# Counting the edges of a graph layer by tiles instead of by windows

## The chip, the cores and the metric

The kernel runs on one core of a Trainium2 chip. The metric is the device time of one launch in microseconds (us). TensorE, VectorE, ScalarE and GpSimd work side by side and order themselves by semaphores; SyncE (SP) only issues DMAs.

## The reference

1250 nodes with 512 features; 21,250 edges, sorted by `dst`. A softmax over each node's edges weighs its neighbours, then a spline layer, a residual and a layer norm follow. Cut to what matters here:

```python
s = HW @ a[:OUT_F, 0];  t = HW @ a[OUT_F:, 0]          # HW = h @ W
e = leaky_relu(s[row] + t[col])                        # row = src, col = dst
m = segment_max(e, row);  ex = exp(e - m[row]);  den = segment_sum(ex, row)
agg = segment_sum((ex / den[row])[:, None] * h[col], row)
out = silu(agg) @ base_w.T + einsum('nip,oip->no', b_splines(agg), spline_w)
return layernorm(x + out)
```

## The kernel before

The softmax is dense. The kernel counts how often each pair (src, dst) occurs, as a matrix C of 1250 x 1250 (src in 128 partitions x 10 groups j, dst along the columns), with Z a second matrix that is large where C is zero. Then `greatest(j)` (L601) takes for each src the largest t among its neighbours, ScalarE makes the exponentials for all pairs, `weigh` multiplies by C, TensorE transposes and aggregates with x, and after that come 36 units of matmuls of the spline layer (L1113), which fill the time from about 170 us on. This document is about what stands ahead of `greatest(0)`.

**The count.** The edges, sorted by dst, lie in 168 tiles of 128, an edge per partition. C's columns are cut into 40 windows of `DW` = 32 dst, so 320 columns of PSUM (src group x dst). For a window w a fixed run of 7 or 8 tiles, from `FIRST[w]`, is visited: 304 matmuls at L1013, each with a stationary one-hot `still` (edge x 128, L414) and a moving one-hot `oh` (edge x 320, L394). The moving one-hot says src group and dst within a window and is made once for each batch of 8 tiles (`moving`, 21 batches). The stationary one-hot says the low seven bits of src and, in its key, which window the edge belongs to, so that it is zero for edges of other windows; it is made anew for each window (`one_hot_still`, 40 times). Both come from VectorE's `is_equal` of a row of numbers (`im`, `iq`) with keys made from the edges (`mk`, `qk`). Four batches of `oh` and four windows of `still` are held. ScalarE copies each window from PSUM to C (L792) and makes Z (L795); six PSUM banks are in use for windows.

**Tiles left over.** Edges of a window that lie in tiles outside its fixed run are added by a loop on VectorE, TensorE and PSUM bank 7 ahead of `greatest(0)` (L559 to L578). Its trip counts are read from a table that VectorE computes between the one-hots (`least_and_most` to `left_sizes`): least and largest dst of each tile, and from them the tiles that each window still wants. With nothing left over, the loop body runs once.

**s and t.** `w_times_a`, `wa_column` and `st_rows` on TensorE make W a and then two rows, s and t, of 1280 nodes in three chunks (12 matmuls at L989, chunk after chunk, each into partitions 0 and 1 of bank 6). `s_column` turns s into a column; `t_spread` spreads t over all 128 partitions by three matmuls (L1005), which ScalarE copies into `trow`. `greatest(0)` reads trow.

**Order of the work.** It is written out by hand: each engine's program is a loop over windows, with the small pieces of work hung on chosen windows (`WA_AT`, `ST_AT`, `SC_AT`, `TB_AT`, `RG_AT`, `RR_AT`). VectorE also makes `x_low` (L502), ten remainders x - xh, four of them inside the loop and six behind it. GpSimd fills constants at the start, then waits for xT (`s_xt`) and issues two DMAs for `xh` (L362, L363), then waits for the first `greatest` to issue weights (L374). SP issues the loads; its next waiting instruction is also behind the first `greatest`.

```python
for v in range(VIS[w]):
    m = e.matmul(PS[:, w % 6, 0:MV], still[:, w % RH, v, :], oh[:, (FIRST[w] + v) % (RB * TB), :],
                 start=(v == 0), stop=(v == VIS[w] - 1))
```

## Time and profile before

| | |
|---|---|
| time, median of 3 | 429.96 us (428.74 to 430.42) |
| the profiled execution | 430.31 us, of which the span is 428.5 |
| mean granted TensorE clock | 0.979 |
| busy: TensorE, VectorE, ScalarE, GpSimd | 399.4, 367.2, 274.0, 33.1 us |
| start of `greatest(0)` | 76.24 us |

The span runs from the first to the last instruction; the time of a launch is 1.8 us longer. PE is TensorE's matmuls, PEld its weight loads, DVE VectorE, ACT ScalarE, POOL GpSimd. Matmuls overlap their successors, so a group's mean duration is longer than its pace.

### The profile page before, as it was taken

Reading aid. Unit: us, or ns where it says so; the run is one execution under the profiler, and the core shown is the slowest. Engines: PE = TensorE matmul, PEld = TensorE weight load, DVE = VectorE, ACT = ScalarE, POOL = GpSimd, SP = SyncE. Lnnn points to the kernel's source line nnn. Section 1 sums busy time; section 2 is a strip of 40 time slices with the busy share of each in tenths; the row PEclk is TensorE's granted clock in tenths of the full one; section 3 lists DMA queues with packets and bytes.
Section 4 is the critical chain, followed back from the end, with each engine's and each line's share of the span. In section 5 each row is a group of like instructions: output and inputs, shape, how many; then the busy total and the mean of one; then the engine's idle time right before and its main releaser. Section 6 shows DMA issues by size and latency. Waiting matters only on the chain.

```text
span 428.5 us, 5227 instructions
## 1 busy us (share of the span) xinstructions
PE 399.4 (93%) x1881; PEld 306.0 (71%) x1881; DVE 367.2 (86%) x457; ACT 274.0 (64%) x299; POOL 33.1 (8%) x162
## 2 busy tenths in 40 slices
PE   3999995299999999999999999999999999999994
PEld 0436563288888888878778888888777777777772
DVE  7968999997868867799988999989799969999645
ACT  7535675456456659788659586678646785779212
POOL 5100000100000000001100110101011010101000
PEclk9999999589999999999999999999999999999998
DMA  8980000600000000955454636363242346371303
GB/s 265 376 201 2 2 0 0 198 0 2 0 0 2 1 2 6 337 173 144 151 165 134 192 102 194 113 182 89 67 139 50 98 124 194 101 217 50 98 1 115
DMA packets 23452, 45.91 MB, mean 107 GB/s; under 512 B 1831, under 2 KB 2043, under 8 KB 23427
## 3 DMA queue, kind: packets, MB, share of 16 engines
q0 software_dynamic: 11088, 21.44, 18.6%
q1 hardware_dynamic: 12338, 24.14, 17.9%
q8 instruction: 15, 0.25, 0.2%
q14 instruction: 11, 0.08, 0.1%
HBM read 43.02 MB, written 2.56 MB: 106 GB/s over the span
## 4 chain that ended last, share of the span: by engine, by line
PE 54%; issue 29%; DVE 9%; POOL 3%; DMA 3%; ACT 0%; DVEq 0%; POOLq 0%
PE PS L1113 24%; PE PS L1069 17%; PE PS L1013 5%; POOL wh L374 3%; PE PS L1052 3%; DVE still L414 2%; DMA wh<-in_splT 2%; PE PS L989 2%; DVE oh L394 1%; DVE xl L502 1%; PE PS L968 1%; PE PS L1079 1%; DVE wl L593 1%; DMA ei<-in_edges 1%; DVE ex L629 0%
## 5 line engine op out<-in xcount | busy, mean ns | idle before, releaser
L1113 PE MATMUL PS<-wh,s 128*128 128x512 f32 (+1 forms) x720 | 225.2, 392 | 2.3 <-ACT s L884 1.1
L1113 PEld LDWEIGHTS PS<-wh,s 128*128 128x128 f32 (+1 forms) x720 | 133.4, 185 | 36.4 <-ACT s L884 3.5
L1113 PE MATMUL PS<-wl,s 128*128 128x512 f32 (+1 forms) x360 | 141.1, 392 | 0.0
L884 ACT ACTIVATE s<-v 128x1280 fp32r<-128x1280 f32 (+1 forms) x32 | 40.0, 1250 | 63.9 <-DVE v L701 58.9
L1113 PEld LDWEIGHTS PS<-wl,s 128*128 128x128 f32 (+1 forms) x360 | 66.8, 185 | 15.2
L1013 PE MATMUL PS<-oh,still 128*128 128x320 bf16 x304 | 45.4, 304 | 9.9 <-DVE still L414 7.9
L695 DVE SCALAR_TENSOR_TENSOR v<-v,v 128x1280 f32<-128x1280 f32 (+1 forms) x32 | 46.5, 1454 | 4.8 <-ACT v L870 4.8
L1013 PEld LDWEIGHTS PS<-oh,still 128*128 128x128 bf16 x304 | 28.8, 99 | 29.6 <-DVE still L414 9.6
L701 DVE SCALAR_TENSOR_TENSOR v<-v,v 128x1280 f32<-128x1280 f32 (+1 forms) x32 | 46.8, 1461 | 3.3
L711 DVE SCALAR_TENSOR_TENSOR s<-v,s 128x1280 fp32r<-128x1280 f32 (+1 forms) x32 | 46.5, 1454 | 0.6 <-ACT s L884 0.6
L697 DVE SCALAR_TENSOR_TENSOR v<-v,v 128x1280 f32<-128x1280 f32 (+1 forms) x32 | 46.5, 1454 | 0.0
L867 ACT ACTIVATE v<-xt,bias 128x1280 f32<-128x1280 f32 (+1 forms) x32 | 42.9, 1342 | 3.5 <-DVE s L711 2.1
L374 POOL DMA_DIRECT2D wh<-in_splT x32 | 22.8, 714 | 279.8 <-PE PS L1113 170.6
L870 ACT ACTIVATE v<-v,bias 128x1280 f32<-128x1280 f32 (+1 forms) x32 | 42.4, 1326 | 0.0
L868 ACT ACTIVATE v<-xt,bias 128x1280 f32<-128x1280 f32 (+1 forms) x32 | 42.4, 1325 | 0.0
L593 DVE TENSOR_TENSOR wl<-wring,wh 128x1024 fp32r<-128x1024 f32 x24 | 29.2, 1221 | 10.4 <-issue 10.4
L394 DVE TENSOR_TENSOR oh<-im,mk 128x2560 bf16<-128x2560 f16 x21 | 31.0, 1478 | 0.1
L414 DVE TENSOR_TENSOR still<-iq,qk 128x1024 bf16<-128x1024 uint16 (+1 forms) x40 | 25.4, 653 | 5.9 <-PE PS L1013 5.9
L792 ACT CAST C<-PS 128x320 uint16<-128x320 f32 x40 | 17.0, 425 | 20.1 <-PE PS L1013 19.5
L652 DVE TENSOR_TENSOR pl<-PS,ph 128x1280 fp32r<-128x1280 f32 (+2 forms) x11 | 15.1, 1368 | 14.7 <-ACT ph L833 14.7
L1069 PE MATMUL PS<-xh,ph 128*128 128x512 f32 x100 | 27.6, 425 | 0.0
L833 ACT CAST ph<-PS 128x1280 fp32r<-128x1280 f32 (+2 forms) x11 | 12.4, 1132 | 21.4 <-PE PS L1052 21.4
(125 smaller groups left out, 374.4 us busy)
## 6 DMA issues: line engine op xcount, KB each, us to landing
wh<-in_splT POOLq DMA_DIRECT2D x32, 512.0 KB, 4.5
wring<-in_splT SPq DMA_DIRECT2D x21, 512.0 KB, 4.4
xt<-in_xT SPq DMA_DIRECT2D x1, 2500.0 KB, 11.6
xn<-in_x SPq DMA_DIRECT2D x1, 2304.0 KB
xh<-in_x POOLq DMA_DIRECT2D x1, 2304.0 KB, 13.3
out<-xr SPq DMA_DIRECT2D x9, 256.0 KB
wh<-in_baseT POOLq DMA_DIRECT2D x4, 512.0 KB, 5.3
wring<-in_baseT SPq DMA_DIRECT2D x3, 512.0 KB, 4.1
```

Source lines behind the costliest of these rows:

```text
L374: e.dma_start(wh[u % NWS][:, :, :], w_source(u)).then_inc(s_wh[u % NWS], 16)
L695: e.scalar_tensor_tensor(out=ba, in0=bw, scalar=2.0, in1=ba, op0=ALU.subtract, op1=ALU.mult, reverse0=True).then_inc(s_a3, 1)
L697: e.scalar_tensor_tensor(out=bq, in0=bw, scalar=2.0, in1=bq, op0=ALU.subtract, op1=ALU.mult).then_inc(s_b3, 1)
L701: e.scalar_tensor_tensor(out=bw, in0=bq, scalar=2 / 3, in1=ba, op0=ALU.add, op1=ALU.min).then_inc(s_spl, 1)
L711: e.scalar_tensor_tensor(out=parts(sl, u), in0=bufs(u)[0], scalar=0.0, in1=parts(sh, u).bitcast(F32), op0=ALU.max, op1=ALU.subtract).then_ ...
L867: e.activation(bw, agg_in, ACT.Abs, bias=bias[:, q - 1:q], scale=2.5).then_inc(s_abs, 1)
L868: e.activation(bq, agg_in, ACT.Square, bias=bias[:, NP + q - 1:NP + q], scale=2.5 * sq2).then_inc(s_q2, 1)
L870: e.activation(ba, bw, ACT.Square, bias=bias[:, 2 * NP:2 * NP + 1], scale=-sq6).then_inc(s_a2, 1)
L884: e.activation(parts(sh, u), bufs(u)[0], ACT.Relu).then_inc(s_shi, 1)
L1013: m = e.matmul(PS[:, w % 6, 0:MV], still[:, w % RH, v, :], oh[:, (FIRST[w] + v) % (RB * TB), :], start=(v == 0), stop=(v == VIS[w] - 1))
L1069: m = e.matmul(PS[:, 5 + j % 2, :], pp[0:r, j % 3, place(j, t), :], xs[0:r, t, :], start=(i == 0 and t == 0), stop=(i == 2 and t == NT - 1))
L1113: m = e.matmul(PS[0:rows(w), w % 8, :], sx[:, ic, tl * 128:tl * 128 + rows(w)], wx[:, ic, :], start=first and n == 0, stop=last and n == 2)
```

## The change

The windows of the output become 25 of 50 dst (500 columns of PSUM, ordered dst x src group, so column = 10 x dst + group). A tile of edges is counted once: its moving one-hot covers a constant stretch of columns around `middle(t)`, `REACH` columns to either side (90 to 160), and the matmul goes to those columns of one window, or is split in two at a window's border. The stationary one-hot is of the low seven bits of src alone and is made once for each batch. Since no matmul covers a whole window, a matmul with zeros (`cleared`) opens each. Keys relative to the middle of the tile (`mk`) take the place of those relative to a window.

The table of left-over tiles is computed by GpSimd in a chain of 29 steps (`s_tab`), of which VectorE does three (two reductions of the tiles' ends, one reduction at batch 10, one scan at batch 13) and reads the result at batch 17. Ahead of it GpSimd makes keys for left-over edges in ten steps (`s_left`). Both stand behind its xh DMAs. A tile is left over if its first or last dst lies outside its stretch.

`st_rows` puts the three chunks into partitions 0, 32 and 64 of one bank, after batches 7 to 10, with one contraction chunk each time; ScalarE copies them to `strow`, and three DMAs on SP's queue, ahead of its weights, copy the rows of t from there to all partitions of `trow`. The remainders of x start at batch 16.

```diff
-DW = 32
-ND = RP // DW
-MV = NT * DW
+DW = 50
+ND = N // DW
+CW = DW * NT
+MV = LW * NT
 TB = 8
 NB = NC // TB
+NV = NC - 1
 RB = 4
-VIS = [8 if ND // 5 <= w < ND - ND // 5 else 7 for w in range(ND)]
-FIRST = [min(max(((2 * w + 1) * DW * PER_NODE // 2 + 64 - 64 * VIS[w]) // 128, 0), NC - VIS[w]) for w in range(ND)]
-NR = 2 * ND
+MID, PER_TILE, PER_BATCH = 42, 75, 602
+REACH = [5 * (18, 22, 24, 26, 28, 30, 30, 32, 32, 32, 32)[min(b, NB - 1 - b)] for b in range(NB)]
+def middle(t):
+    return MID + PER_BATCH * (t // TB) + PER_TILE * (t % TB)
+def stretches(t):
+    lo, hi = max(middle(t) - REACH[t // TB], 0), min(middle(t) + REACH[t // TB], ND * CW)
+    return [(w, max(lo, CW * w), min(hi, CW * w + CW)) for w in range(lo // CW, (hi - 1) // CW + 1)]
+FIRST_TILE = [min(t for t in range(NV) if w in [p[0] for p in stretches(t)]) for w in range(ND)]
+LAST_TILE = [max(t for t in range(NV) if w in [p[0] for p in stretches(t)]) for w in range(ND)]
...
+            for k, (lo, hi) in enumerate(TCH):
+                hi = min(hi, N)
+                if k == 0:
+                    e.wait_ge(s_srow, 3)
+                e.dma_start(trow[:, lo:hi], strow[32 * k + 1:32 * k + 2, 0:hi - lo].unsqueeze(1).broadcast_to([1, 128, hi - lo])
+                            ).then_inc(s_trow, 16)
...
+            e.wait_ge(s_edge, 16)
+            e.wait_ge(s_bits, 2)
+            e.wait_ge(s_setup, SETUP["reach"])
+            e.tensor_copy(left_place[:, :], ei[:, 1, :]).then_inc(s_left, 1)
+            e.tensor_copy(left_in[:, :], et[:, 0, :]).then_inc(s_left, 1)
...
+            e.tensor_tensor(left_key[:, :, :], left_place[:, :].unsqueeze(2).broadcast_to([128, NCP, 2]),
+                            left_in[:, :].unsqueeze(2).broadcast_to([128, NCP, 2]), ALU.add).then_inc(s_left, 1)
...
+            e.wait_ge(s_ends_r, 1)
+            e.tensor_scalar(wf[:, :, 0:NC], ends[:, :, :], 1 / LW, (1 - LW) / (2 * LW), ALU.mult, ALU.add).then_inc(s_tab, 1)
+            for k in range(2):
+                e.wait_ge(s_tab, k + 1)
+                e.tensor_scalar(wf[:, :, 0:NC], wf[:, :, 0:NC], (WHOLE, -WHOLE)[k], None, ALU.add).then_inc(s_tab, 1)
...
+            e.tensor_scalar(rest[:, 0:NC], n_of[:, :], 1.0, None, ALU.max).then_inc(s_tab, 1)
+            for k in range(2):
+                e.tensor_tensor(ways[:, k, :], ways[:, k, :], out_of[:, :], ALU.mult).then_inc(s_tab, 1)
+            e.wait_ge(s_least, 1)
+            e.tensor_scalar(tu[:, 2:3], tu[:, 0:1], -1.0, float(NC), ALU.mult, ALU.add).then_inc(s_tab, 1)
+            e.wait_ge(s_tab, 16)
...
+            e.wait_ge(s_scan, 1)
+            e.tensor_tensor(here[:, 1, :], wf[:, 0, :], upto_rest[:, 0:NC + 1], ALU.subtract).then_inc(s_tab, 1)
+            e.wait_ge(s_tab, 23)
+            e.tensor_copy(r_rest[:, :, 0], here[:, 1, :]).then_inc(s_tab, 1)
+            for k in range(2):
+                e.tensor_copy(r_rest[:, :, 1 + k], upto_rest[:, k:k + NC + 1]).then_inc(s_tab, 1)
+            e.tensor_copy(r_size[:, 0:1], tu[:, 2:3]).then_inc(s_tab, 1)
+            e.tensor_copy(r_size[:, 1:2], tu[:, 4:5]).then_inc(s_tab, 1)
+            e.tensor_copy(r_size[:, 2:3], upto_rest[:, NC + 1:]).then_inc(s_tab, 1)
...
             def moving(b):
-                c0 = TB * b
+                h = REACH[b]
                 if b >= RB:
-                    e.wait_ge(s_cw, last_window(b - RB) + 1)
+                    e.wait_ge(s_ct, done(b - RB))
                 e.tensor_tensor(
-                    oh[:, c0 % (RB * TB):c0 % (RB * TB) + TB, :].rearrange("p k (m b) -> p k m b", b=2),
-                    im[:, :].rearrange("p (m b) -> p m b", b=2).unsqueeze(1).broadcast_to([128, TB, MV // 2, 2]),
-                    mk[:, c0:c0 + TB, :].unsqueeze(2).broadcast_to([128, TB, MV // 2, 2]),
+                    oh[:, b % RB, :, 0:2 * h].rearrange("p k (m b) -> p k m b", b=2),
+                    im[:, MV // 2 - h:MV // 2 + h].rearrange("p (m b) -> p m b", b=2).unsqueeze(1)
+                    .broadcast_to([128, TB, h, 2]),
+                    mk[:, TB * b:TB * b + TB, :].unsqueeze(2).broadcast_to([128, TB, h, 2]),
                     ALU.is_equal).then_inc(s_mv, 1)
...
-            def one_hot_still(w):
-                k = VIS[w]
-                if w >= RH:
-                    e.wait_ge(s_cw, w - RH + 1)
-                e.wait_ge(s_iq, w.bit_length())
-                e.tensor_tensor(still[:, w % RH, 0:k, :].rearrange("p k (m b) -> p k m b", b=2),
-                                places_of(slice(128 * w, 128 * w + 128), k), lows_of(FIRST[w], k), ALU.is_equal
+            def places_of(k):
+                return im[:, MV // 2:MV // 2 + 128].rearrange("p (m b) -> p m b", b=2).unsqueeze(1).broadcast_to(
+                    [128, k, 64, 2])
+            def one_hot_still(b):
+                e.tensor_tensor(still[:, b % RB, :, :].rearrange("p k (m b) -> p k m b", b=2), places_of(TB),
+                                lk[:, TB * b:TB * b + TB, :].unsqueeze(2).broadcast_to([128, TB, 64, 2]), ALU.is_equal
                                 ).then_inc(s_head, 1)
...
+            e.tensor_scalar(et[:, 0, :], ei[:, 0, :], 7, None, ALU.arith_shift_right).then_inc(s_bits, 1)
+            e.tensor_scalar(et[:, 1, :], ei[:, 0, :], 127, None, ALU.bitwise_and).then_inc(s_bits, 1)
+            e.wait_ge(s_setup, SETUP["mid"])
+            e.wait_ge(s_bits, 1)
+            e.tensor_tensor(left_hi[:, :], et[:, 0, :], mid[:, :], ALU.subtract).then_inc(s_hc, 1)
+            e.wait_ge(s_hc, 1)
+            e.scalar_tensor_tensor(out=mk[:, :, :], in0=ei[:, 1, :].unsqueeze(2).broadcast_to([128, NCP, 2]),
+                                   scalar=float(NT), in1=left_hi[:, :].unsqueeze(2).broadcast_to([128, NCP, 2]),
+                                   op0=ALU.mult, op1=ALU.add).then_inc(s_mk, 1)
+            e.wait_ge(s_mk, 1)
+            for b in range(NB):
+                moving(b)
+                if b == 0:
+                    e.wait_ge(s_lk, 1)
+                one_hot_still(b)
+                if b == 1:
+                    e.wait_ge(s_dn, 16)
+                    e.tensor_reduce(mm[0:NBLK, :, 0], dn[0:NBLK, :, :], AX.X, ALU.min).then_inc(s_ends, 1)
+                    e.tensor_reduce(mm[0:NBLK, :, 1], dn[0:NBLK, :, :], AX.X, ALU.max).then_inc(s_ends, 1)
+                if b == LEAST_AT:
+                    e.wait_ge(s_tab, 15)
+                    e.tensor_reduce(tu[:, 0:2], ways[:, :, :], AX.X, ALU.max).then_inc(s_least, 1)
+                if b == SCAN_AT:
+                    e.wait_ge(s_tab, 22)
+                    e.wait_ge(s_setup, SETUP["begin"])
+                    e.tensor_tensor_scan(upto_rest[:, 1:], rest[:, :], zero[:, :], 0.0, ALU.add, ALU.add
+                                         ).then_inc(s_scan, 1)
+                if b == SIZES_AT:
+                    e.wait_ge(s_tab, TABLE)
+                    first, behind = loaded(e, r_size, 0, 2, 0, NC + 1)
+                if b in X_LOW_AT:
+                    x_low(X_LOW_AT[b] - 1)
+            for k in range(len(X_LOW_AT), NT):
+                x_low(k)
+            e.wait_ge(s_left, 10)
...
+            e.wait_ge(s_bits, 2)
+            e.copy(lk[:, :, :], et[:, 1, :].unsqueeze(2).broadcast_to([128, NCP, 2])).then_inc(s_lk, 1)
+            def st_rows():
+                e.wait_ge(s_sr, 1)
+                for k, (lo, hi) in enumerate(TCH):
+                    e.copy(strow[32 * k:32 * k + 2, 0:hi - lo], PS[32 * k:32 * k + 2, 6, 0:hi - lo]).then_inc(s_srow, 1)
+            def evacuate_counts(w):
+                ps = PS[:, w % 6, 0:CW].rearrange("p (b a) -> p a b", a=NT)
                 d = slice(DW * w, DW * w + DW)
-                e.wait_ge(s_cw, w + 1)
+                e.wait_ge(s_ct, LAST_TILE[w] + 1)
...
-                m.then_inc(s_sr, 1)
+                for k, (lo, hi) in enumerate(TCH):
+                    m = e.matmul(PS[32 * k:32 * k + 2, 6, 0:hi - lo], wa[:, it, :], xt0[:, it, lo:hi], start=(it == 0),
+                                 stop=(it == 3))
+                if it == 3:
+                    m.then_inc(s_sr, 1)
...
-            for w in range(ND):
-                if w >= 6:
-                    e.wait_ge(s_hole, w - 5)
-                e.wait_ge(s_head, w + 1)
-                for v in range(VIS[w]):
-                    m = e.matmul(PS[:, w % 6, 0:MV], still[:, w % RH, v, :], oh[:, (FIRST[w] + v) % (RB * TB), :],
-                                 start=(v == 0), stop=(v == VIS[w] - 1))
-                m.then_inc(s_cw, 1)
-                if w in WA_AT:
-                    w_times_a(WA_AT.index(w))
-                if w == WT_AT:
...
+            def cleared(w):
+                e.matmul(PS[:, w % 6, 0:CW], nought[:, 0:128], nought[:, :], start=True, stop=False)
+            e.wait_ge(s_setup, SETUP["nought"])
+            for w in range(6):
+                cleared(w)
+            for b in range(NB):
+                e.wait_ge(s_mv, b + 1)
+                e.wait_ge(s_head, b + 1)
+                for t in range(TB * b, done(b)):
+                    o = middle(t) - REACH[b]
+                    for w, lo, hi in stretches(t):
+                        if w >= 6 and t == FIRST_TILE[w]:
+                            e.wait_ge(s_hole, w - 5)
+                            cleared(w)
+                        m = e.matmul(PS[:, w % 6, lo - CW * w:hi - CW * w], still[:, b % RB, t % TB, :],
+                                     oh[:, b % RB, t % TB, lo - o:hi - o], start=False, stop=(t == LAST_TILE[w]))
+                    m.then_inc(s_ct, 1)
+                if b in WA_AT:
+                    w_times_a(WA_AT.index(b))
```

## Rows read from the trace of the kernel before

**Rows 1.** table of stretches: length, busy us (x) of PE, PEld, DVE, ACT, POOL; granted clock; DMA.
```profile
50.00:60.00 10.00, 10.00 (x75) 7.17 (x74) 10.00 (x15) 7.44 (x19) 0.00 (x0) 1.00 0.00 0
60.00:70.00 10.00, 7.11 (x51) 4.55 (x50) 10.00 (x15) 5.82 (x14) 0.00 (x0) 1.00 0.00 0
70.00:80.00 10.00, 2.17 (x15) 1.21 (x13) 8.68 (x21) 4.04 (x9) 1.46 (x2) 0.81 0.10 26
80.00:90.00 10.00, 7.13 (x22) 5.73 (x23) 9.58 (x24) 7.07 (x8) 0.00 (x0) 0.51 0.56 186
```

**Rows 2.** groups by line, 0 to 100 us: busy, mean ns, idle time before them.
```profile
L1013 PE MATMUL PS<-oh,still 128*128 128x320 bf16 x304 | 45.4, 304 | 9.9 <-DVE still L414 7.9 <-ACT Z L795 2.0
...
L1013 PEld LDWEIGHTS PS<-oh,still 128*128 128x128 bf16 x304 | 28.8, 99 | 29.6 <-DVE still L414 9.6 <-ACT Z L795 5.3 <-issue 3.8
```

**Rows 3.** groups by shape, VectorE alone, 0 to 76 us.
```profile
L394 DVE TENSOR_TENSOR oh<-im,mk 128x2560 bf16<-128x2560 f16 x21 | 31.0, 1478 | 0.1
L414 DVE TENSOR_TENSOR still<-iq,qk 128x1024 bf16<-128x1024 uint16 x24 | 16.1, 682 | 5.9 <-PE PS L1013 5.9
L414 DVE TENSOR_TENSOR still<-iq,qk 128x896 bf16<-128x896 uint16 x16 | 9.4, 610 | 0.0
...
L421 DVE TENSOR_REDUCE mm<-dn 84x2 f32<-84x256 int32 x1 | 0.4, 407 | 0.0
...
L567 DVE TENSOR_TENSOR one_moving<-im,mk 128x320 bf16<-128x320 f16 x1 | 0.3, 306 | 0.0
```

**Rows 4.** timeline, VectorE's first one-hots: start us, duration us, what.
```profile
4.91 1.49 DVE L394 TENSOR_TENSOR oh<-im,mk 128x2560 bf16<-128x2560 f16 x1
...
6.32 0.62 DVE L414 TENSOR_TENSOR still<-iq,qk 128x896 bf16<-128x896 uint16 x1
```

**Rows 5.** timeline, GpSimd at the start.
```profile
0.84 0.40 POOL L322 IOTA im<- 128x320 f16 x1 [0.39 <-POOLq L1165]
...
1.78 0.17 POOL L332 IOTA wr<- 128x40 f32 x1
...
2.34 0.29 POOL L337 TENSOR_SCALAR_AFFINE_SELECT ident<-ident 128x128 f32<-128x128 f32 x1 [0.16 <-POOL ident L335]
...
4.92 0.09 POOL L351 MEMSET visits<- 1x1 f32 x1
...
14.62 1.16 POOL L362 DMA_DIRECT2D xh<-in_x  x1 [8.16 <-DMA xt<-in_xT]
...
15.77 0.58 POOL L363 DMA_DIRECT2D xh<-in_x  x1
```

**Rows 6.** timeline, 22 to 70 us: s and t, a copy, a run of count matmuls.
```profile
25.20 0.57 ACT L786 COPY trow<-PS 2x512 f32<-2x512 f32 x1 [2.67 <-PE PS L989]
...
28.46 3.60 PE L989 MATMUL PS<-xt,wa 128*2 128x512 f32 x8
...
49.85 11.99 PE L1013 MATMUL PS<-oh,still 128*128 128x320 bf16 x87
```

**Rows 7.** timeline, the end of the count.
```profile
69.78 0.61 DVE L414 TENSOR_TENSOR still<-iq,qk 128x896 bf16<-128x896 uint16 x1
...
70.31 3.68 DVE L502 TENSOR_TENSOR xl<-xn,xh 128x512 fp32r<-128x512 f32 x6
...
73.92 0.31 DVE L567 TENSOR_TENSOR one_moving<-im,mk 128x320 bf16<-128x320 f16 x1
...
76.24 1.46 DVE L601 CUSTOM_DVE_ANT_0 scrap<-trow,Z 128x1250 bf16<-128x1250 f32 x1 [0.42 <-DVE Z L578]
...
82.17 1.11 PE L1052 MATMUL PS<-ident,ex 128*128 128x128 f32 x4 [7.37 <-DVE ex L632]
```

**Rows 8.** groups by line, ScalarE's two passes over a window.
```profile
L795 ACT ACTIVATE Z<-PS,bias 128x320 bf16<-128x320 f32 x40 | 21.3, 532 | 0.0
L792 ACT CAST C<-PS 128x320 uint16<-128x320 f32 x40 | 17.0, 425 | 20.1 <-PE PS L1013 19.5
```

**Rows 9.** page, bytes per second in 40 slices.
```profile
GB/s 265 376 201 2 2 0 0 198 0 2 0 0 2 1 2 6 337 173 144 151 165 134 192 102 194 113 182 89 67 139 50 98 124 194 101 217 50 98 1 115
```

More of the change, by code:

```diff
@@ L160, in build @@
+        (s_bits, s_hc, s_mk, s_ends, s_least, s_scan, s_mv, s_head, s_ovk, s_ovm, s_ovs, s_ova, s_ovz, s_tmax, s_small, s_top, s_p, s_den, s_rden, s_xlo, s_plo,
          s_a3, s_b3, s_spl, s_slo, s_wlo, s_res, s_bns, s_bna, s_var, s_rstd, s_nb, s_fin) = (
             sem(f"v_{n}") for n in (
-                "bits", "keys", "rng", "rest", "mv", "head", "ovm", "ovs", "ova", "ovz", "tmax", "small", "top", "p", "den", "rden", "xlo", "plo",
+                "bits", "hc", "mk", "ends", "least", "scan", "mv", "head", "ovk", "ovm", "ovs", "ova", "ovz", "tmax", "small", "top", "p", "den", "rden", "xlo", "plo",
@@ L554, in _ @@
-            for w in range(4, NT):
-                x_low(w)
-            e.wait_ge(s_hole, ND)
-            with e.Fori(0, windows) as j:
-                _, (start, n0, n1, w) = nc.values_load_multi_w_load_instructions(
-                    r_rest[0:1, bass.ds(within(j, 0, NR), 1), :].rearrange("p a b -> p (a b)"), engines=[e.engine],
-                    min_val=-NR * NC, max_val=NR * NC, skip_runtime_bounds_check_because=CLAMPED)
-                w = within(w, 0, ND - 1)
-                d = bass.ds(w * DW, DW)
-                with e.Fori(within(n0, 0, NR * NC), within(n1, 1, NR * NC)) as n:
-                    tile = within(n + start, 0, NC)
+            e.tensor_scalar(et[:, 0, :], ei[:, 0, :], 7, None, ALU.arith_shift_right).then_inc(s_bits, 1)
@@ new lines, in _ @@
+            for k in range(len(X_LOW_AT), NT):
+                x_low(k)
+            e.wait_ge(s_left, 10)
+            with e.Fori(first, behind) as j:
+                tile = within(j, 0, NC)
+                _, (start, n0, n1) = nc.values_load_multi_w_load_instructions(
+                    r_rest[0:1, bass.ds(tile, 1), :].rearrange("p a b -> p (a b)"), engines=[e.engine],
+                    min_val=-LND * NC, max_val=LND * NC, skip_runtime_bounds_check_because=CLAMPED)
+                with e.Fori(within(n0, 0, LND * NC), within(n1, 1, LND * NC)) as n:
+                    w = within(n + start, 0, LND - 1)
+                    d = bass.ds(w * LW, LW)
+                    e.tensor_tensor(kk[:, :, :], left_key[:, bass.ds(tile, 1), :], lplace[:, bass.ds(w, 1), :],
+                                    ALU.subtract).then_inc(s_ovk, 1)
+                    e.tensor_tensor(one_still[:, :, :].rearrange("p k (m b) -> p k m b", b=2), places_of(1),
+                                    lk[:, bass.ds(tile, 1), :].unsqueeze(2).broadcast_to([128, 1, 64, 2]), ALU.is_equal
+                                    ).then_inc(s_ovs, 1)
+                    e.wait_ge(s_ovk, n + 1)
@@ L985, in st_rows @@
                     e.wait_ge(s_setup, SETUP["xpad"])
[L986 to L990 removed]
+                for k, (lo, hi) in enumerate(TCH):
+                    m = e.matmul(PS[32 * k:32 * k + 2, 6, 0:hi - lo], wa[:, it, :], xt0[:, it, lo:hi], start=(it == 0),
+                                 stop=(it == 3))
```

435 lines of the change are left out of this document (172 added, 263 removed).

## The prediction

> **What bounds the kernel now.** I read the table of stretches first, then the groups of instructions, then the timeline around both ends of the count. From 50 to 60 us TensorE and VectorE are both busy all the time, from 60 to 70 VectorE still is and TensorE 7.1 of 10, and the granted clock is 1.00, which is 2.4 GHz [rows 1]: the end of the stage is VectorE's. The count (L1013) is 304 matmuls, 45.4 us, all before 72 us [rows 2]. What ends the stage is VectorE's queue: it builds the last stationary one-hot at 69.78, then six remainders of x, then the loop for left-over tiles from 73.92, and `greatest(0)` starts at 76.24 [rows 7]. Everything behind `greatest(0)` hangs on it: TensorE's next work starts at 82.17 [rows 7]. So the question is when `greatest(0)` starts after the change. What follows is the same code on the same data, 428.5 - 76.24 = 352.3 us, and I let it shift rigidly.
>
> VectorE's 73.9 us up to the loop add up so. 21 moving one-hots: 4.91 to 6.32 is 1.41 from start to start of a 1.49 us instruction, so starts lie 0.08 closer than durations [rows 4]; 1478 ns each [rows 3] gives 21 x 1.40 = 29.4. 40 stationary ones: 24 x 0.61 + 16 x 0.54 = 23.3 [rows 3, 4]. Ten remainders of x at 0.61 [rows 7]: 6.1. Waits for TensorE: 5.9 [rows 3]. First one-hot at 4.91 [rows 4]. The remaining 4.3 us are the small instructions of the range table and register loads.
>
> **The change part by part, on VectorE.**
> Moving one-hots: 128x320 takes 306 ns and 128x2560 takes 1478 [rows 3], so 0.523 ns per column and 0.14 fixed, 0.06 of it visible in a pitch. The REACH constants sum to 2900; a batch has 8 tiles of 2 x REACH columns, together 46,400 columns: 24.3 + 21 x 0.06 = 25.5 us, -3.9.
> Stationary ones: they are of the low seven bits of src alone and serve every window, so 21 of 1024 columns: 21 x 0.61 = 12.8, -10.5. This is the largest term.
> The table goes to GpSimd; VectorE keeps two reductions of 0.41 [rows 3], two operations of at most 0.45 and a register load, 1.9 for 4.3: -2.4.
> Waits for TensorE: -5.9, if TensorE keeps up (below).
> Start: two keys fewer, one more dependent step: -0.4. The left-over loop: with the edges that the reference draws, each tile's first and last node lie inside its stretch by at least 26 columns, so no tile is left over and the loop runs once as before, with one more small operation: +0.2.
> Sum -22.9: `greatest(0)` at 53.3, if nothing else is late.
>
> **TensorE.** The stretches cut 167 tiles into 257 matmuls of 46,003 columns. 87 matmuls of 320 columns in 11.99 us are 0.138 each, 0.43 ns per column [rows 6], so 19.8 us; if a piece can't be shorter than the 99 ns of a weight load [rows 2] (167 are), 27.3. To this come 19 clears of 500 columns behind the first six, 4.1. The s and t rows take 3.6 us for eight 512-column steps [rows 6], 8.9 in all before; in three column groups they take a third at best and the same 8.9 at worst. I take the worst: this puts 2.2 us behind each of batches 7 to 10, where VectorE makes a batch in 2.0 and TensorE needs 1.4 to 1.8. With four batches of buffers VectorE then waits some 1.5 us at batch 14, and nothing if the groups run side by side. So 0 to 1.5 us, taken 0.
>
> The Trainium skill, TensorEngine Tiling (Array Packing), Key Properties, says that column tiles run in parallel but that a change of tiling drains the array. No row here has a tiled matmul; by it the rows would take about 3.5 us, which gives the same sum because TensorE is not last.
>
> **ScalarE.** 40 pairs at 425 + 532 ns [rows 8] become 25 of 500 columns. A 512-column copy is 0.57 [rows 6], 0.15 more than 320 columns, so a pair is about 1.25 and all are 31 us for 38. After the last tile it has two windows, 2.5 us, hidden by the remainders of x still to come on VectorE, 9 of which follow batch 17 here. Without that cover it would cost 2.5.
>
> **GpSimd, the wait that is added.** 80 memsets go, but 39 dependent elementwise operations come, on an engine that did none, and behind its two issues for xh, which start at 14.62 once xT has landed and end at 16.35 [rows 5]. VectorE stops at batch 10 until 15 table steps are done; those stand behind the ten for the left-over keys. Behind that waiting instruction are all the one-hots of batches 11 to 20, so TensorE, ScalarE and `greatest(0)` wait too.
> VectorE reaches it at: 4.5 + 1530 x 16 x 0.523 ns + 11 x 0.06 + 11 x 0.61 + 0.8 = 25.5 us.
> GpSimd: no row shows its elementwise operations, so I bound them. Low: iota 0.40 for 320 columns and 0.17 for 40 [rows 5], 0.14 + 0.8 ns per column; the keys are nine of 176 columns and one of 352, 3.0 us, the table seven of 336 and eight of 168, 5.1; dependent steps lie 0.16 apart (the idle time ahead of affine_select [rows 5]), 3.3 for 21. Ready at 16.4 + 11.4 = 27.8. High: two and a half times the cost per column for two inputs, one and a half for one (affine_select, 128 columns in 0.29, is 1.2 ns [rows 5]): 16.0, ready at 32.4. So 2.3 to 6.9 us of stall; I take the middle, 4.6. From below, nothing excludes an engine quick enough for none. The later waits (batches 13 and 17) leave 6 and 7 us for seven operations each and cost nothing at these prices.
>
> **The row of t.** The three matmuls and copies that spread it go, and SP sends it by three DMAs. They are issued when the three copies are done, about 30 to 35 us, and nothing but `greatest(0)` needs them, 20 us on. Covered in the sum, with a rival below.
>
> **Sum.** 53.3 + 4.6 = 57.9 against 76.24: -18.3. The profiled execution took 430.31, 1.8 more than its span and 0.35 above the median shown; 430.31 - 18.3 = 412.0, and 411.7 against the median. I say **412**, with 409.5 to 414.5 as this case's own range. TensorE's cold stretch remains: it sat idle for 7.37 us ahead of 82.17 [rows 7] and the clock of 80 to 90 was 0.51, near the 1.2 GHz level [rows 1]; after the change it idles from the last tile to `greatest(0)` and 6 us beyond, at least as long.
>
> **Rivals.**
> (a) No stall at all: GpSimd is done by 25.5. 430.3 - 22.9 = 407.4. For it: a memset of GpSimd passes in 0.09 [rows 5]. Chance 0.10.
> (b) GpSimd's and VectorE's instructions take turns. If an operation of one holds back the other, GpSimd's chain lies in VectorE's time. From 16.4, VectorE has 9.1 us of work before batch 10 ends, nine instructions, with nine of GpSimd's between; then 16 remain, alone, at d + 0.16 each for a mean d; then 25.3 us to the loop with 14 more between, and 2.4 for the loop. `greatest(0)` at 55.8 + 39 d: for d between 0.28 and 0.45 (my bounds above) 66.7 to 73.4, time 421 to 427.5. Against it: a memset at 4.92 passes in 0.09 under VectorE's first one-hot [rows 4, 5], but it reads nothing. For it: the one GpSimd operation that reads SBUF, affine_select at 2.34, ran with VectorE idle, so no row speaks [rows 5]. Chance 0.20. The Trainium skill, SBUF — State Buffer, Who interferes with whom, states just this: a VectorE operation with two SBUF inputs and a GpSimd operation that reads SBUF exclude each other for a whole instruction. No row of this trace tests it.
> (c) The row of t lands last. All 128 copies of a chunk are read from one partition. In the profile the 16 DMA engines moved 376 GB/s in their fullest slices, 23.5 per engine [rows 9]; if one source partition yields no more than that, 1250 x 4 x 128 bytes take 27 us, from 35 to 62 or 64: 416 to 418. Against: they may be spread. Chance 0.13.
> (d) Slower: (b) with GpSimd dearer. `greatest(0)` passes 76.24 when 39 d reaches 20.4, so the point from which it decides is d = 0.52 us per operation, with the taking of turns; at 0.75 it is 85, and the time 439. For it: 39 operations have to pass one after another, most with a wait between; against: every compute row of GpSimd is 0.40 or less [rows 5]. Chance 0.09. The Trainium skill, GPSIMD Engine Reference, Elementwise side-by-side cycle accounting, gives 2.6 cycles per element for two inputs; an estimate from it for 336 columns is 0.73 us plus dispatch, which is my high bound rather than this case.
> (e) The count is not what bounds: TensorE's narrow pieces pace it, each with its load and start. At 0.14 for each of the 257 it is 36 us beside 16 of other work, 52 from 6 us on: end near 60, 414. Chance 0.05, inside the range.
>
> **How the numbers follow.** Forecast 0.43, (a) 0.10, (b) 0.20, (c) 0.13, (d) 0.09, (e) 0.05. The range is 407 to 426: it leaves out (d) and the dearest end of (b). Half a per cent, 2.1 us, is about what a measurement of this kernel can tell from no change. Slower by more: (d), 0.08; within: the rest of (d) and the top of (b), 0.05; faster 0.87.
>
> **What would show it.** Right: 21 stationary one-hots near 0.68 us; VectorE idle once for 2 to 7 us near 25, released by GpSimd; GpSimd's table operations at 0.3 to 0.7 us; `greatest(0)` near 58. (b) shows as one-hots that take longer or start later wherever GpSimd works, (c) as `greatest(0)` waiting for the DMA of trow. The forecast is wrong if VectorE waits for TensorE in batches 11 to 20, or if the stretch behind `greatest(0)` is not 352 us long.

## The result, and the profile after

| | before | after |
|---|---|---|
| time, median of 5 | 429.20 us (428.74 to 430.42) | 432.58 us (431.69 to 433.28) |
| span of the profiled execution | 428.5 | 431.0 |
| mean granted TensorE clock | 0.979 | 0.950 |
| start of `greatest(0)` | 76.24 | 78.54 |
| behind it, to the end of the span | 352.3 | 352.5 |

The ratio is 1.0063, with a 95% interval of 1.0042 to 1.0085: slower by 0.4 to 0.9%, where 412 us was forecast. What follows `greatest(0)` moved rigidly, so the miss lies wholly ahead of it: 78.54 instead of 57.9, 20.6 us.

VectorE's groups of instructions up to 80 us in the kernel after answer to [rows 3]: busy time, mean ns of one, idle time before them.

```profile
L491 DVE TENSOR_TENSOR oh<-im,mk 128x2560 bf16<-128x2560 f16 (+6 forms) x21 | 27.2, 1296 | 0.0
L505 DVE TENSOR_TENSOR still<-im,lk 128x1024 bf16<-128x1024 f16 x21 | 14.2, 678 | 0.0
L514 DVE TENSOR_TENSOR xl<-xn,xh 128x512 fp32r<-128x512 f32 (+1 forms) x10 | 6.4, 683 | 2.8 <-POOL r_size L471 2.8
L519 DVE TENSOR_SCALAR et<-ei 128x176 int32<-128x176 int32 x1 | 1.5, 1496 | 3.1 <-DMA ei<-in_edges 3.1
...
L546 DVE TENSOR_TENSOR_SCAN upto_rest<-rest,zero 1x169 f32<-1x169 f32 x1 | 0.5, 497 | 3.4 <-POOL rest L462 3.4
L542 DVE TENSOR_REDUCE tu<-ways 1x2 f32<-1x336 f32 x1 | 0.5, 490 | 18.0 <-POOL ways L449 18.0
```

The one-hots are as forecast: 21 stationary ones of 678 ns, 21 moving ones of 1296 ns in the mean. In the last column stand three waits for GpSimd, 18.0 + 3.4 + 2.8 = 24.2 us; one of 4.6 was forecast. The first small instruction, L519, took 1.50 us. From the table of stretches (columns as in [rows 1]):

```profile
20.00:30.00 10.00, 10.00 (x90) 5.47 (x88) 6.92 (x8) 6.46 (x13) 9.65 (x6) 1.00 1.37 256
30.00:40.00 10.00, 1.66 (x15) 0.51 (x12) 0.00 (x0) 3.29 (x7) 9.16 (x12) 0.82 0.51 16
40.00:50.00 10.00, 2.48 (x13) 1.47 (x13) 5.12 (x6) 0.00 (x0) 8.97 (x9) 0.50 0.91 27
50.00:60.00 10.00, 9.02 (x62) 5.95 (x62) 6.63 (x8) 5.21 (x12) 9.05 (x8) 0.65 0.43 23
```

From 30 to 40 us VectorE runs nothing at all and GpSimd works 9.16 of 10; TensorE idles, and its granted clock is 0.82 in that stretch and 0.50 of 2.4 GHz, the 1.2 GHz level, in the next. What GpSimd did, in the timeline (start us, duration us, what):

```profile
15.86 0.62 POOL L396 DMA_DIRECT2D xh<-in_x  x1
16.47 10.65 POOL L402 CAST left<-ei 128x176 f32<-128x176 int32 x1
27.07 0.33 POOL L403 CAST left<-et 128x176 f32<-128x176 int32 x1
27.50 0.69 POOL L405 TENSOR_SCALAR left<-left 128x176 f32<-128x176 f32 x1
28.27 0.57 POOL L407 TENSOR_TENSOR left<-left,left 128x176 f32<-128x176 f32 x1
...
37.96 0.88 POOL L433 TENSOR_TENSOR over<-over,reach 1x336 f32<-1x336 f32 x1
38.93 1.05 POOL L436 TENSOR_SCALAR over<-over 1x336 f32<-1x336 f32 x1
...
45.46 5.97 POOL L451 TENSOR_SCALAR tu<-tu 1x1 f32<-1x1 f32 x1 [0.61 <-DVE tu L542]
51.52 0.22 POOL L453 TENSOR_SCALAR tu<-tu 1x1 f32<-1x1 f32 x1
...
55.33 8.34 POOL L464 TENSOR_TENSOR here<-wf,upto_rest 1x169 f32<-1x169 f32 x1 [0.61 <-DVE upto_rest L546]
63.74 0.40 POOL L466 CAST r_rest<-here 1x169 int32<-1x169 f32 x1
```

Two copies of the same 128x176 stand behind each other at 10.65 and 0.33 us. The same engine needs 5.97 us for a single number at L451 and 0.22 for the next. The long ones end when VectorE stops; its own timeline:

```profile
24.84 1.48 DVE L491 TENSOR_TENSOR oh<-im,mk 128x2560 bf16<-128x2560 f16 x1
26.24 0.68 DVE L505 TENSOR_TENSOR still<-im,lk 128x1024 bf16<-128x1024 f16 x1
44.88 0.49 DVE L542 TENSOR_REDUCE tu<-ways 1x2 f32<-1x336 f32 x1 [17.96 <-POOL ways L449]
45.30 1.47 DVE L491 TENSOR_TENSOR oh<-im,mk 128x2560 bf16<-128x2560 f16 x1
...
78.54 1.46 DVE L604 CUSTOM_DVE_ANT_0 scrap<-trow,Z 128x1250 bf16<-128x1250 f32 x1 [0.42 <-DVE Z L581]
```

VectorE ran out at 26.92, and L402 ended at 27.12. VectorE's one-hots in that time are not longer (1.48 and 0.68) and have no gaps. The rest of the first wait is GpSimd's own prices: 0.5 to 0.9 us for most operations of 168 to 352 columns, 24 of them in the 17.8 us from 27.07 to 44.88.

### The profile page after: what moved, and what is told of

It is laid out like the page before. It is cut to its first block, busy times and chain, and to the rows that moved or that the text cites. A ratio compares the mean times of both kernels' runs of the same rounds, so it can differ in the third digit from the quotient of the medians.

```text
span 431.0 us, 5055 instructions
## 1 busy us (share of the span) xinstructions
PE 384.4 (89%) x1853; PEld 299.1 (69%) x1853; DVE 351.4 (82%) x416; ACT 261.8 (61%) x264; POOL 80.3 (19%) x164
## 4 chain that ended last, share of the span: by engine, by line
issue 39%; PE 35%; POOL 15%; DVE 5%; DMA 4%; DVEq 1%; ACT 0%; SPq 0%; POOLq 0%
PE PS L1072 16%; PE PS L1116 15%; POOL wh L482 4%; DMA xt<-in_xT 3%; PE PS L1055 3%; POOL left L402 2%; POOL here L464 2%; POOL tu L451 1%; DMA wh<-in_splT 1%; DVE xl L514 1%; PE PS L1082 1%; POOL wf L428 0%; DVE ex L632 0%; DVE scrap L604 0%; DVE v L704 0%
## 5 line engine op out<-in xcount | busy, mean ns | idle before, releaser
L1020 PE MATMUL PS<-oh,still 128*128 128x320 bf16 (+37 forms) x257 | 32.7, 278 | 24.9 <-DVE still L505 24.9
L1020 PEld LDWEIGHTS PS<-oh,still 128*128 128x128 bf16 x257 | 22.0, 112 | 39.6 <-DVE oh L491 30.1
L596 DVE TENSOR_TENSOR wl<-wring,wh 128x1024 fp32r<-128x1024 f32 x24 | 29.2, 1221 | 11.5 <-issue 11.4
L791 ACT CAST C<-PS 128x500 uint16<-128x500 f32 x25 | 14.4, 576 | 38.5 <-PE PS L1020 38.4
L491 DVE TENSOR_TENSOR oh<-im,mk 128x2560 bf16<-128x2560 f16 (+6 forms) x21 | 27.2, 1296 | 0.0
L1072 PE MATMUL PS<-xl,ph 128*128 128x512 f32 x100 | 25.4, 399 | 0.0
```

Source lines behind the costliest of these rows:

```text
L1020: m = e.matmul(PS[:, w % 6, lo - CW * w:hi - CW * w], still[:, b % RB, t % TB, :], oh[:, b % RB, t % TB, lo - o:hi - o], start=False, stop ...
L1072: m = e.matmul(PS[:, 5 + j % 2, :], pp[0:r, j % 3, place(j, t), :], xs[0:r, t, :], start=(i == 0 and t == 0), stop=(i == 2 and t == NT - 1))
```

## The experiments

Four theories for the long GpSimd operations are named in the expectations. **S**: a GpSimd operation that reads SBUF is held back as long as VectorE issues two-input operations back to back. **T**: the two take turns, rival (b). **L**: a one-time cost of GpSimd's first arithmetic. **P** came up later, for a register load: it is held up by DMAs that read an SBUF partition. Two more, **Q** and **H**, are stated where they are tested (e5, e11). Ratios are to runs of the kernel before on the same chip, medians 429.3 to 429.7, with 95% intervals.

### e1_late

```diff
-        ENDS_AT, LEAST_AT, SCAN_AT, SIZES_AT = 3, 10, 13, 17
+        ENDS_AT, LEAST_AT, SCAN_AT, SIZES_AT = 3, 17, 18, 19
```

> The changed kernel with VectorE's three meetings with GpSimd's table moved from batches 10, 13 and 17 to 17, 18 and 19, so that VectorE works without a wait for GpSimd from 6 to about 41 us. Theory S (starved): a GpSimd operation that reads SBUF waits until VectorE's queue runs dry, not for one instruction. Then the first key operation (L402), 10.65 us in the changed kernel, lasts from 16.5 until VectorE stops at batch 17, some 24 us, the rest of the chain runs after it, and greatest(0) is at about 77 to 80 us, the time 431 to 434. Theory T (turns, as in my rival b): L402 takes at most 2 us and each of the 25 operations ahead of the meeting costs VectorE about 0.5 us; batch 17 ends at about 53. Theory L (a long GpSimd instruction is a one-time cost of GpSimd's own, such as a first use): L402 stays at 10.65 us, the chain is ready at 44.9 as before, and with the waits gone greatest(0) comes at about 62, the time 416.

431.82 us, ratio 1.0044 (1.0023 to 1.0064), `greatest(0)` at 78.59. GpSimd's timeline:

```profile
16.86 24.30 POOL L402 CAST left<-ei 128x176 f32<-128x176 int32 x1
41.11 0.32 POOL L403 CAST left<-et 128x176 f32<-128x176 int32 x1
```

VectorE stops seven batches later, and the same copy takes 24.30 us instead of 10.65, again until VectorE's stop (40.27 + 0.69). A fixed cost (L) would have left it at 10.65, turns (T) at 2 us at most. Nor is the copy held by the xh transfer that GpSimd issues just ahead of it. In the kernel after that transfer landed near 27.6, about when the copy ended, so the one trace could not tell; in e1 both its parts had landed by 29.4, and the copy ran on to 41.2. The wait at batch 17 is 17.9 us: cover of seven batches more hid nothing.

### e2_no_table and e3_no_table_pe

e2 leaves out GpSimd's 39 operations and VectorE's two that belong to them; constants stand in place of keys and table. The 39 are ten for the keys and 29 for the table; the section on the change counts VectorE's reductions and scan among the 29, but they come on top. e3 besides spreads t as the kernel before did, by TensorE and ScalarE:

```diff
-                e.dma_start(trow[:, lo:hi], strow[32 * k + 1:32 * k + 2, ...].broadcast_to([1, 128, hi - lo]))
+                e.matmul(PS[:, 6, 0:hi - lo], ident[q:q + 2, q + 1:q + 2].broadcast_to([2, 128]), strow[q:q + 2, ...])
+                    e.copy(trow[:, lo:min(hi, N)], PS[:, 6, 0:min(hi, N) - lo])     # ScalarE, batches 13, 15, 17
```

> The changed kernel without the 39 GpSimd operations of keys and table and without VectorE's two that belong to them (the reductions of the tiles' ends stay); the loop's sizes are constants, one turn. This takes out all that the waits for GpSimd cost. My sum said greatest(0) at 53.3, with the later start that the profile after shows 54.7. The row of t in the changed kernel landed 12 to 22 us after its issues at 33.4 to 34.6, so by 57: if that is the next bound (my rival c), greatest(0) starts at 56 to 58 and waits for the DMA of trow; the time 410 to 412. If the DMAs are quicker without the other traffic, 408.5. If the waits for GpSimd were not what cost the time, it stays near 432.

> As the run before it, and the row of t is spread by TensorE and copied by ScalarE at batches 13, 15 and 17, as the kernel before did, in place of the three DMAs. If the DMA of trow bounds e2_no_table, this one is 1 to 3 us faster, greatest(0) at about 54.7, time 408.5; if it does not, both are the same within 0.5.

e2: 418.27, ratio 0.9726 (0.9685 to 0.9768), `greatest(0)` at 64.89. e3: 406.22, ratio 0.9455 (0.9427 to 0.9484), `greatest(0)` at 53.38. So e2 missed its expectation by some 7 us. e3 took that back and came out 2.3 us below its own 408.5. In e2 VectorE's timeline has a wait of a new kind:

```profile
40.28 0.69 DVE L435 TENSOR_TENSOR still<-im,lk 128x1024 bf16<-128x1024 f16 x1
52.26 0.69 DVE L444 TENSOR_TENSOR xl<-xn,xh 128x512 fp32r<-128x512 f32 x1 [11.30 <-issue]
```

"issue" means that no semaphore held it. The registers for the left-over loop are loaded just there (batch 17), on VectorE's sequencer (DVEq); the tile r_size in e2 (duration min/median/max in ns, start in us):

```profile
L225 DVEq TENSOR_LOAD <-r_size x1: 14348/14348/14348, 37.8 to 37.8; - x1
```

and in e3:

```profile
L225 DVEq TENSOR_LOAD <-r_size x1: 770/770/770, 36.8 to 36.8; - x1
```

The load of a few numbers takes 14.35 us in place of 0.77 and ends at 52.2. It is not VectorE's alone: TensorE's sequencer loads the same tile in 7.61 us in e2 and 0.48 in e3. In e2 the three DMAs of trow were issued from 33.94 and landed 11.9, 20.1 and 22.2 us later.

### e4_dve_table

The same 39 operations, one or two behind each one-hot on VectorE; GpSimd has none.

> The changed kernel with the same 39 operations, in the same order, on VectorE, one or two behind each one-hot of batches 6 to 15; GpSimd does none. Theories S and T: the waits go and VectorE pays 39 x 0.2 to 0.25 us, 8 to 10 us: greatest(0) at 63 to 65, time 417 to 419, faster than both kernels. If the operations themselves are as dear on VectorE as on GpSimd (0.6 each), 23 us and 432.

423.78, ratio 0.9870 (0.9839 to 0.9902), `greatest(0)` at 70.44. The operations cost VectorE 0.13 to 0.51 us each, 9.8 in all, which was expected; the 7.03 us of "issue" behind a load of 11.63 us were not. It missed by about what the load costs.

### e5_load_early

e2 with the loop's bounds read at batch 10 instead of 17, when no DMA of trow is under way.

> e2_no_table with its reads of r_size into registers (VectorE's and TensorE's) moved from batch 17 to batch 10, ahead of the DMAs of trow. In e2 VectorE stood 11.3 us (41.0 to 52.3) and its register load of r_size, from partition 0, took 14.35 us; with no DMA of trow in e3 the same load took 0.77. Theory P: a register load from SBUF is held up by the three DMAs, which all read from one partition of SBUF for every destination (1, 33, 65). Then the 11.3 us at batch 17 go and greatest(0) comes at 54 to 58: the DMAs are done by 56.5, and the load of r_rest for the loop, issued near 44, may be held until some 54. Time 407 to 411. Theory Q: the DMAs slow VectorE or its instruction supply as such, wherever the load is: VectorE still stands some 11 us between 38 and 52, time 416 to 418.

411.20, ratio 0.9568 (0.9538 to 0.9598), `greatest(0)` at 58.40, just above both of theory P's ranges. The load of r_size is back at 0.77. But the loop body's own load, r_rest, is issued while the DMAs run:

```profile
L481 DVEq TENSOR_LOAD <-r_rest x1: 11861/11861/11861, 43.5 to 43.5; - x1
```

and VectorE waits 4.74 us, "issue", for its end at 55.4. The same loads are short without the DMAs and long beside them wherever they stand. That is P as far as it can be told apart here; whether it is the partition that both read, or the queue, was not separated.

### e6_bystander

e3 with a GpSimd chain on a tile of its own that nobody waits for: six iota (write only), four tensor_scalar (read and write), six iota, all 128x176.

> e3_no_table_pe (no key or table operations on GpSimd, t spread by TensorE) with a chain on GpSimd behind its xh DMAs that nobody reads or waits for: six iotas of 128x176, which write SBUF and read none, then four tensor_scalar of 128x176, which read it, then six iotas. Theory S: the iotas pass at 0.4 us each from 16.5, the first tensor_scalar lasts until VectorE's queue runs dry near 51, over 30 us, the other three take 0.7 each then; VectorE's one-hots keep 1.48 and 0.68 us and the time stays within 0.5 of e3's 406.2, so that GpSimd alone pays. Theory T (turns): every GpSimd operation waits for one VectorE instruction, none over 2 us, and VectorE is 3 us later. If the iotas are held as well, what counts is not reading.

406.35, ratio 0.9461 (0.9437 to 0.9486), `greatest(0)` at 53.62. GpSimd's timeline:

```profile
16.10 2.05 POOL L402 IOTA scr<- 128x176 f32 x6
18.25 35.50 POOL L406 TENSOR_SCALAR scr<-scr 128x176 f32<-128x176 f32 x4
53.82 2.01 POOL L409 IOTA scr<- 128x176 f32 x6
```

and the group of four by itself (min/median/max ns):

```profile
L406 POOL TENSOR_SCALAR scr<-scr x4: 647/647/33313, 18.2 to 53.1; 128x176 f32<-128x176 f32 x4
```

Writes pass beside VectorE's one-hots at 0.28 us each. The first operation that reads takes 33.3 us, until 51.6; VectorE's one-hots and remainders had ended at 51.0. The other three take 0.65. VectorE loses nothing measurable (53.62 against 53.38). This is S, without a table, a wait or a first use of the engine.

### e7_dve_table_pe

e4 with t spread as in e3.

> e4_dve_table (all keys and table on VectorE) with t spread by TensorE as in e3. e4 lost 7.0 us at its register load (11.6 us) and had batch 17 at 48.4 before it where e3 had 38.5, so the 41 operations cost VectorE 9.8 us. Theory P: without the DMAs of trow the load takes 0.8, greatest(0) is at 53.4 + 9.8 = 63.2 and the time 416 to 416.5.

417.05, ratio 0.9718 (0.9690 to 0.9746), `greatest(0)` at 63.35; the load is at 0.78. Both causes away, the price of keys and table on VectorE remains: 63.35 - 53.38 = 10.0.

### e8_fused_pe

e7 with keys in 5 operations and table in 18, by using VectorE's three-operand form, and four copies on ScalarE. It computes all that the kernel after does.

```diff
-    e.tensor_tensor(over[:, :, :], ends[:, :, :], sign[:, :, :], ALU.mult)
-    e.tensor_tensor(over[:, :, :], over[:, :, :], mids[:, :, :], ALU.add)
+    e.scalar_tensor_tensor(out=over[:, 0, :], in0=ends[:, 0, :], scalar=-10.0, in1=mids[:, 0, :], op0=ALU.mult, op1=ALU.add)
```

> e7 with the same table and keys in fewer steps: 5 operations for the keys in place of 10 and 18 in place of 31 for the table on VectorE (products and sums joined, both comparisons joined with their products), and 4 copies on ScalarE at batch 14. Nothing of the computation is left out. VectorE's cost by the durations of e4: 5 x 0.25 + 18 x 0.2 = 5 us, so greatest(0) at 58 to 59 and the time 411 to 412, 4% below the kernel before.

412.65, ratio 0.9611 (0.9585 to 0.9637), `greatest(0)` at 59.53: 6.2 us behind e3's for the 5 expected. It beats both kernels.

### e9_table_first

The kernel after with GpSimd's ten key operations moved behind the table. Nothing needs them before the left-over loop.

> The changed kernel with GpSimd's ten key operations moved behind its table, so that they no longer stand between VectorE's wait at batch 10 and the table. The table's first 15 steps took 11.5 us in the changed kernel (33.35 to 44.88). Theory S: the first of them is held until VectorE stops at 26.9, the wait at batch 10 ends at 38.5 in place of 44.9, but the keys, which the loop for left-over tiles waits for, get no turn while VectorE runs and start only when it stops ahead of the loop near 70; ten operations of 0.65 with their waits follow, so the 6.4 us come back and greatest(0) is at 77 to 79, the time within 1 of the changed kernel (431 to 433). Theory T (turns) or any theory in which the keys run beside VectorE: greatest(0) at 72, time 426.

427.22, ratio 0.9938 (0.9916 to 0.9961). The wait at batch 10 fell from 17.96 to 11.43 us, as expected, and a different operation, the first of the table, was now held for 9.65 us. But `greatest(0)` came at 74.42, between the two expectations and earlier than S alone allows, since the keys ran beside VectorE. GpSimd's timeline:

```profile
59.17 0.68 POOL L456 TENSOR_SCALAR left<-left 128x176 f32<-128x176 f32 x1
59.94 0.66 POOL L458 TENSOR_TENSOR left<-left,left 128x176 f32<-128x176 f32 x1
60.67 1.36 POOL L460 TENSOR_TENSOR left<-left,mid 128x176 f32<-128x176 f32 x1
```

and VectorE's:

```profile
59.49 0.69 DVE L515 TENSOR_TENSOR xl<-xn,xh 128x512 fp32r<-128x512 f32 x1 [2.76 <-POOL r_size L447]
60.10 1.51 DVE L492 TENSOR_TENSOR oh<-im,mk 128x1920 bf16<-128x1920 f16 x1
61.53 1.05 DVE L506 TENSOR_TENSOR still<-im,lk 128x1024 bf16<-128x1024 f16 x1
```

Here both pay: 1.36 for GpSimd's 0.56, 1.51 and 1.05 for VectorE's 1.15 and 0.68. From 59.49 to its six last remainders VectorE needs 8.80 us where the kernel after needed 6.50 for the same instructions (66.03 to 72.53). That is 2.3 for the seven key operations from L458 on, 0.33 each in the mean, at most 0.65. So 6.5 us came back and 2.3 were paid. When VectorE started at 59.49, GpSimd was already at work (L456); in all the held cases VectorE was running when GpSimd came.

### e10_order

e8 with GpSimd's constants of one partition ahead of 39 memsets of 128 partitions (bias and reach_col).

> e8_fused_pe with GpSimd's constants in another order: those on one partition (sign, mids, ways, turn, rest, reach: memsets and iotas) come ahead, those on 128 partitions (bias, reach_col, lplace) behind. In all kernels with the change VectorE's first operation (a tensor_scalar of 128x176) took 1.5 to 1.7 us in place of 0.26 and ended when GpSimd's run of memsets on 128 partitions did. If that run held it, it is back at 0.26 to 0.3, the one-hots and greatest(0) start 1.2 to 1.4 us earlier and the time is 411.3 for 412.65. If it is any run of GpSimd's writes, also on one partition, it stays at 1.5 or grows to 3 and the time stays.

412.21, ratio 0.9602 (0.9580 to 0.9624), where 411.3 was expected. In the kernel after, the run of memsets on 128 partitions ended at 4.60, beside L519's end at 4.71:

```profile
3.78 0.82 POOL L372 MEMSET reach_col<- 128x8 f32 x22
```

VectorE's timeline at the start in e10:

```profile
3.16 0.37 DVE L438 TENSOR_SCALAR et<-ei 128x176 int32<-128x176 int32 x1 [3.04 <-DMA ei<-in_edges]
...
4.71 0.91 DVE L410 TENSOR_TENSOR oh<-im,mk 128x1440 bf16<-128x1440 f16 x1
...
17.93 0.32 DVE L470 TENSOR_SCALAR wf<-ends 1x336 f32<-1x336 f32 x1 [0.72 <-ACT ends L803]
```

The first instruction is back from 1.50 to 0.37 us and the one-hots start 1.35 earlier, but `greatest(0)` only 0.55 (58.98). VectorE now reaches the table's first step before ScalarE has the tiles' ends, and 0.72 goes there. In time it can't be told from e8; both are the best complete kernels measured.

### e11_turns_free and e12_turns_chained

e3 with one iota and sixteen tensor_scalar (one input each) on GpSimd; VectorE waits once, ahead of batch 8, so that GpSimd is at work when it starts again. In e11 an operation waits for the one before the last, in e12 for the last.

```diff
+            for n in range(16):
+                e.wait_ge(s_left, max(1, n))          # e12: n + 1
+                e.tensor_scalar(scr[:, 1 + n % 2, :], scr[:, 0, :], float(NT), None, ALU.mult)
...
+                if b == 8:
+                    e.wait_ge(s_left, 3)
```

> Kernel of e3_no_table_pe (span 404.7, greatest(0) at 53.4) with a GpSimd chain that nobody needs afterwards: one iota and sixteen tensor_scalar of 128x176 that read SBUF. VectorE waits once, ahead of batch 8, for the first two of them (held until then), so that GpSimd is already at work when VectorE starts again; each further operation waits only for the one before the last. Both theories: about 1.5 us for the pause. Theory 'the one in possession keeps its turn' (H): the other fourteen run beside VectorE, 1.3 to 1.5 us each instead of .65, over some 20 us, and make one-hots beside them .35 to .45 us longer each: 14 x .4 to .65 = 6 to 9 us, greatest(0) at 60.5 to 64. Theory 'GpSimd is held whenever VectorE runs back to back' (S): the third is held until VectorE runs dry near 52, VectorE pays only the pause, greatest(0) at 54.5 to 55.5.

> As e11_turns_free, but each GpSimd operation waits for the one directly before it, as the chain of the changed kernel does. H with possession lost in the gap between two operations: one or two run beside VectorE, then the next is held until VectorE's next stop or near 52, greatest(0) at 54.5 to 56. H with possession kept over the gap: as e11, 60.5 to 64, with operations a little longer apart. S: as in e11, third operation held, 54.5 to 55.5. In table_first's ten key operations, which were chained, possession was kept, so the second is what I expect.

e11: 409.88, ratio 0.9542 (0.9504 to 0.9580). e12: 410.73, ratio 0.9564 (0.9532 to 0.9595). GpSimd's group in e11 and then in e12:

```profile
L403 POOL TENSOR_SCALAR scr<-scr x16: 647/1014/3702, 17.7 to 37.8; 128x176 f32<-128x176 f32 x16
```

```profile
L403 POOL TENSOR_SCALAR scr<-scr x16: 649/1012/4088, 17.3 to 37.8; 128x176 f32<-128x176 f32 x16
```

VectorE in e11:

```profile
20.20 0.68 DVE L436 TENSOR_TENSOR still<-im,lk 128x1024 bf16<-128x1024 f16 x1
22.16 1.49 DVE L422 TENSOR_TENSOR oh<-im,mk 128x2560 bf16<-128x2560 f16 x1 [1.28 <-POOL scr L403]
23.57 0.82 DVE L436 TENSOR_TENSOR still<-im,lk 128x1024 bf16<-128x1024 f16 x1
24.31 1.61 DVE L422 TENSOR_TENSOR oh<-im,mk 128x2560 bf16<-128x2560 f16 x1
...
39.28 0.68 DVE L436 TENSOR_TENSOR still<-im,lk 128x1024 bf16<-128x1024 f16 x1
...
56.70 1.46 DVE L528 CUSTOM_DVE_ANT_0 scrap<-trow,Z 128x1250 bf16<-128x1250 f32 x1 [0.42 <-DVE Z L505]
```

The first of the sixteen is held until VectorE's stop (3.70, 4.09). The fourteen behind the pause all run beside VectorE, the last of them at 37.8, about one for each one-hot; VectorE's instructions become 0.13 longer (0.82, 1.61) and are back at 0.68 when the chain is done. S in its strict form, the third held until 52, is refuted in both (e12's timeline has the same pace), and a wait between two operations makes no difference to who gets turns. My price for a turn was three to five times too high: `greatest(0)` at 56.70 is 3.3 behind e3's, 1.3 of it the pause and 14 x 0.13 = 1.8 the turns, where 6 to 9 had been expected.

## Why the prediction was wrong, point by point

**The step that failed** is "GpSimd, the wait that is added". It had GpSimd working from 16.4 on, beside VectorE, and done at 27.8 to 32.4. The runs show two faults in it.

*The chain did not start.* The engine was ready at 16.47 and did nothing until VectorE stopped at batch 10, so that none of the 10.5 us before the stall was used. e1 and e6 show that this is no property of the operation, the table or the engine's first use: it lasts as long as VectorE runs, 10.65, 24.3 or 33.3 us. The prediction had the right two engines in rival (b), but with the wrong outcome: it made both pay for each other by turns, while here one paid everything. The condition that (b) did not have is which engine was at work first (e9, e11). The Trainium skill, SBUF — State Buffer, Who interferes with whom, says that a two-input VectorE operation contends with a GpSimd operation that reads SBUF and not with one that only writes; e6 agrees (0.28 against 33.3 us). It also says, of VectorE's two-port mode, that whoever issues first gets the pair for the whole instruction. The runs go beyond that sentence: ten VectorE instructions started past the held copy in the kernel after (16.5 to 26.9 us). Read as one instruction's wait, the rule would have held the copy for one one-hot, at most 1.5 us. In all the held cases VectorE's stream was of two-input operations; no run tests a stream with one input.

*The price was too low.* With nothing in the way the 24 operations took 17.8 us, to which the first copy comes; my bounds for all 25 were 11.4 and 16.0. I had let tensor_scalar be cheaper than tensor_tensor; at 336 columns it is 1.05 against 0.88, with one exception (L425, a multiplication and an addition in one, 0.47). An estimate from these rows: without any hold, and at the prices measured while VectorE stood still, the chain would have been ready at 16.5 + 0.3 + 17.8 = 34.6, a stall of 7.7 at 26.9. So of the 13.4 us by which the stall exceeded its 4.6, about 3.1 are price and 10.3 are the hold.

**The later waits** (batches 13 and 17), costed at nothing, took 3.4 and 2.8. Their first operations, L451 and L464, were held 5.97 and 8.34 us in the same way; with those gone the steps around them fit into the 6 and 7 us that the prediction gave them.

**The start** was forecast 0.4 earlier and came 1.15 later, 6.06 against 4.91 [rows 4]. The edge keys' first step ran 1.50 us, for 0.25 in the kernel before, beside GpSimd's memsets of 128 partitions; e10 shows the cause (0.37 with other memsets there). "80 memsets go" had counted them, but not asked which remain and where.

These make 10.3 + 3.1 + 6.2 + 1.5 = 21.1 against the 20.6 us missed; the 0.5 left over lies in small terms that were not followed up.

**What held.** Moving one-hots: 27.2 busy, less 21 x 0.08 = 25.5, as forecast. Stationary ones: 21 x 0.60 = 12.6 for 12.8. VectorE's sum: e3, which has neither hold nor table, starts `greatest(0)` at 53.38 against 53.3 in the prediction; that is partly luck, since e3 also leaves out two VectorE operations of 0.5, beside a start that is 1.5 later. TensorE was never last: in e3 no one-hot waits for it, and rival (e) falls. The s and t rows ran in three column groups side by side, from the timeline of the kernel after:

```profile
23.20 1.03 PE L985 MATMUL PS<-xt,wa 128*2 128x512 f32 x6
```

1.03 us per batch, for the 2.2 that the worst case had, answering to [rows 6]. Rival (a)'s number, 407.4, is near what the kernel gives when the table is gone and TensorE spreads t (406.2); with the table gone and the DMAs kept it gives 418.3 (e2), so a quick GpSimd alone would not have reached it. And the stretch behind `greatest(0)` was 352.5 for 352.3: from 70 to 80 us TensorE's granted clock was 0.67 for 0.81 before, but from 80 to 90 it was 0.50 for 0.51 [rows 1], so the stage starts cold in both.

**The rivals.** (d), slower by turns above 0.52 us each, had chance 0.09 for the sign that came; its mechanism is not the one that acted, and the turns that were measured cost VectorE 0.13 (e11) to 0.33 us in the mean (e9), less than its 0.52. (c) had about the right price. From 30 to 60 us nearly all that moved was the copies of t,

```profile
DMA packets 434, 0.66 MB, mean 22 GB/s; under 512 B 48, under 2 KB 176, under 8 KB 432
```

but that mean counts the ends of the window, where nothing moved. The first copy was issued at 33.4 and the last landed near 57, so the 0.64 MB went at 27 GB/s, for the 23.5 and the landing at 62 that (c) assumed. In the kernel after that is hidden by the stall. Without the stall the copies do cost time, but not where (c) looked: in e2 the register load held VectorE 11.3 us, and the time was 418.3 without any GpSimd work; in e4, where VectorE reaches batch 17 at 48.4, the load still cost 7.0. So the forecast of 412 would most likely have failed on this second cause, which the prediction did not have, had GpSimd's chain been as quick as forecast; no run has just that.
